# One common power for the three normalisations of an attention step on GpSimd

## What is computed

```python
def _layernorm(x, axis=-1, eps=1e-05):
    m = jnp.mean(x, axis=axis, keepdims=True)
    v = jnp.var(x, axis=axis, keepdims=True)
    return (x - m) / jnp.sqrt(v + eps)

x = x + _L0_attn_ref(_layernorm(x), ...)        # 16 heads of 8, queries = keys = values
x = x + _L0_xattn_ref(_layernorm(x), ctx, ctx)  # scores / sqrt(8), softmax over 64 keys
x = x + _L0_ffn_ref(_layernorm(x), ...)         # 7 experts, top 1, and a shared one
```

## Time and profile before

| | |
|---|---|
| median of three runs | 415.33 us (414.82 to 415.68) |
| span of the profiled execution | 427.0 us |
| PE busy | 404.4 us (95%) |
| DVE busy | 305.1 us (71%) |
| ACT busy | 298.5 us (70%) |
| POOL busy | 284.8 us (67%) |
| attention pipeline, full | about 40 to 222 us |
| drain of the attention, routing | about 222 to 270 us |
| experts | from 270 us on |

### The profile page before, as it was taken

The page is one execution under the profiler, slowest core; times in us unless marked ns, Lnnn a source line. Parts: engine busy times, 40 slices in busy tenths (PEclk is TensorE's granted clock), DMA queues, the critical chain, the costliest instruction groups (busy, mean ns, idle before and its releaser), DMA issues.

```text
span 427.0 us, 16199 instructions
## 1 busy us (share of the span) xinstructions
PE 404.4 (95%) x5545; PEld 312.9 (73%) x5546; DVE 305.1 (71%) x791; ACT 298.5 (70%) x684; POOL 284.8 (67%) x476
## 2 busy tenths in 40 slices
PE   7989999999998999999999898969999999999997
PEld 4646666666665666666665667959988999999996
DVE  7868999999998998999999787713333444444444
ACT  7659999999998999999998685302213466666651
POOL 8757788878887888888888423665664463444442
PEclk9999999999999999999999999996999999999999
DMA  6254566767676667765444300021113255430001
GB/s 104 43 85 64 87 103 108 109 110 121 120 124 117 114 123 126 143 101 84 60 63 43 35 2 2 27 81 58 69 69 90 67 133 139 131 104 27 27 32 52
DMA packets 176324, 35.22 MB, mean 82 GB/s; under 512 B 145587, under 2 KB 174646, under 8 KB 176256
## 3 DMA queue, kind: packets, MB, share of 16 engines
q1 hardware_dynamic: 71296, 21.43, 23.1%
q10 hardware_dynamic: 102144, 6.81, 15.2%
q0 software_dynamic: 2816, 6.10, 4.1%
HBM read 20.86 MB, written 15.67 MB: 86 GB/s over the span
## 4 chain that ended last, share of the span: by engine, by line
PE 68%; DMA 10%; issue 6%; DVE 6%; ACT 3%; SPq 2%; POOL 2%; another core or an unknown queue 2%; DVEq 0%; ACTq 0%; POOLq 0%
PE psum L867 15%; PE psum L659 12%; PE psum L668 12%; PE psum L973 8%; PE psum L680 7%; DMA orow<-attention_out 3%; DMA attention_out<-on_s 3%; PE psum L690 3%; SPq L198 2%; DMA ring<-sorted_rows 2%; PE psum L763 2%; PE psum L802 2%; PE psum L758 1%; PE psum L809 1%
## 5 line engine op out<-in xcount | busy, mean ns | idle before, releaser
L1583 DVE TENSOR_TENSOR gT<-gT,psum 128x384 f32<-128x384 f32 x66 | 36.5, 553 | 77.5 <-PE psum L867 34.4
L1263 ACT ACTIVATE gT<-psum 128x384 f32<-128x384 f32 x70 | 33.6, 488 | 58.4 <-PE psum L867 36.9
L620 POOL DMA_INDIRECT out<-yrow,token x38 | 37.1, 975 | 41.2 <-DVE yrow L1718 22.0
L973 PE MATMUL psum<-wdn_sb,gT 128*128 (+1 forms) x420 | 60.2, 280 | 4.0 <-DVE rows_all L1597 2.2
L479 POOL TENSOR_TENSOR k_s<-pT,hmask_sb 128x1024 f32<-128x1024 f32 x32 | 61.0, 1906 | 0.9 <-ACT pT L1137 0.8
L973 PEld LDWEIGHTS psum<-wdn_sb,gT 128*128 128x128 f32 x420 | 53.3, 195 | 5.7 <-issue 2.7
L867 PE MATMUL psum<-fhT,wtile 128*128 128x128 f32 x456 | 57.2, 275 | 0.3 <-ACT wtile L1292 0.3
L867 PE MATMUL psum<-hT_all,wup_sb 128*128 128x128 f32 x384 | 50.9, 283 | 5.0 <-issue 3.8
L867 PEld LDWEIGHTS psum<-fhT,wtile 128*128 128x128 f32 x456 | 53.9, 192 | 0.5 <-ACT wtile L1292 0.5
L867 PEld LDWEIGHTS psum<-hT_all,wup_sb 128*128 128x128 f32 x384 | 47.7, 198 | 6.0 <-issue 4.8
L1065 ACT ACTIVATE pr_x<-pr_x,rs 128x512 f32<-128x512 f32 x60 | 43.0, 722 | 8.2 <-DVE pr_x L1368 7.0
(11 more groups left out here) (193 smaller groups left out, 872.0 us busy)
## 6 DMA issues: line engine op xcount, KB each, us to landing
sorted_rows<-nowhere_row SPq DMA_DIRECT2D x38, 130.0 KB, 3.6
ring<-sorted_rows SPq DMA_DIRECT2D x30, 130.0 KB
wup_sb<-in_wup SPq DMA_DIRECT2D x14, 176.0 KB, 3.0
orow<-attention_out SPq DMA_DIRECT2D x31, 64.0 KB
ring<-in_ctxv ACTq DMA_DIRECT2D x60, 32.0 KB, 3.7
cross_keys<-in_ctxk ACTq DMA_DIRECT2D x14, 128.0 KB, 3.7
ring<-cross_keys SPq DMA_DIRECT2D x112, 16.0 KB
rows_all<-in_x ACTq DMA_DIRECT2D x10, 128.0 KB, 3.9
```

The lines of the kernel that those rows point to most:

```text
L620: pool.indirect_dma_start(out=out, out_offset=bass.IndirectOffsetOnAxis(ap=token[p][:, 0:1], axis=0), in_=yrow[p][:, :], in_offset=None, b ...
L973: last = nc.tensor.matmul(ps_y[p], gT[place_of(n) if isinstance(n, int) and n < FIRST else p][:, c, :], wdn_sb[:, expert, c, :], start=(c ...
```

## The change

The three norms share one addition of epsilon and one power on POOL, both over three columns. The s column has its place in the common one in the step in which DVE makes its variance ("pv_x" of POOL's step), which is later in POOL's order than the separate pair stood by one common block. The separate ve and power of s (L503, L508) leave the step, and with them the factor 8 in the variance: xn_s is multiplied by 8 ** -0.5 instead, in the same instruction. nmean leaves too: L450 becomes (row - mean) * rs, reading the mean in `mv`. ACT's cross exponential waits for the common power. DVE's variances wait for the uses of the same pair two units before, since the mean is now read to the end. In the drain one of the hand-written powers takes s along (unit 28), the last three units keep powers of their own, and the buffer numbers follow.

```diff
-        mhalf = sb("mhalf", [P, 2])
+        mhalf = sb("mhalf", [P, 3])
-        nmean = [sb(f"nmean{i}", [P, 3]) for i in range(2)]
@@ normed
-                nc.gpsimd.tensor_scalar(dst, x_all[:, u, :], nmean[i][:, NORM[k]:NORM[k] + 1], rs[i][:, NORM[k]:NORM[k] + 1],
-                                        ALU.add, ALU.mult).then_inc(sem(f"{k}_xn"), 1)
+                nc.gpsimd.tensor_scalar(dst, x_all[:, u, :], mv[i][:, NORM[k], 0:1], rs[i][:, NORM[k]:NORM[k] + 1],
+                                        ALU.subtract, ALU.mult).then_inc(sem(f"{k}_xn"), 1)
@@ POOL body
+                if live("norm"):
+                    pool.wait_ge(sem("p_mv"), at(u["norm"]))
+                if live("st_x"):
+                    pool.wait_ge(sem("x_mv"), at(u["st_x"]))
+                if live("pv_x"):
+                    pool.wait_ge(sem("s_mv"), at(u["pv_x"]))
+                nc.gpsimd.tensor_scalar(ve[:], mv[i][:, :, 1], EPS, None, ALU.add).then_inc(sem("px_ve"), 1)
...
-                    nc.gpsimd.tensor_scalar(nmean[i][:, 1:3], mv[i][:, 1:3, 0], -1.0, None, ALU.mult).then_inc(sem("px_mean"), 1)
...
+                if u["pv_x"] >= 2:
+                    pool.wait_ge(sem("x_exp"), G * (u["pv_x"] - 1))
+                pool.wait_ge(sem("px_ve"), px_turn(t))
+                nc.gpsimd.tensor_tensor(rs[i][:], ve[:], mhalf[:], ALU.pow).then_inc(sem("px_rs"), 1)
...
-                    nc.gpsimd.tensor_scalar(xn["s"][:], x_all[:, u["q"], :], mv[i][:, 0, 0:1], None,
-                                            ALU.subtract).then_inc(sem("s_xn"), 1)
+                    nc.gpsimd.tensor_scalar(xn["s"][:], x_all[:, u["q"], :], mv[1 - i][:, 0, 0:1], float(DK) ** -0.5,
+                                            ALU.subtract, ALU.mult).then_inc(sem("s_xn"), 1)
...
-                    nc.gpsimd.tensor_scalar(ve[:, 0:1], mv[i][:, 0, 1:2], EPS, float(DK), ALU.add, ALU.mult).then_inc(sem("s_ve"), 1)
...
-                    nc.gpsimd.tensor_tensor(rs[i][:, 0:1], ve[:, 0:1], mhalf[:, 0:1], ALU.pow).then_inc(sem("s_rs"), 1)
@@ POOL drain, roots_x
+                nc.gpsimd.tensor_scalar(ve[:, columns], mv[i][:, columns, 1], EPS, None, ALU.add).then_inc(sem("px_ve"), 1)
...
-            roots_x(33, U - 6)
+            roots_x(33, U - 6, U - 4)
             finish_x(33, U - 6)
-            centred(U + 1, U - 3)
-            root_s(33, U - 3)
+            centred(34, U - 3)
+            root_s(34, U - 3)
@@ ACT exp
-                if k == "x":
-                    act.wait_ge(sem("s_rs"), at(u))
+                if k == "x" and u < U - 3:
+                    act.wait_ge(sem("px_rs"), px_turn(u + LAG["pv_x"]))
+                elif k == "x":
+                    act.wait_ge(sem("s_rs"), u - (U - 3) + 1)
@@ DVE mean_variance
-                if k == "s" and u >= 2:
-                    dve.wait_ge(sem("s_ve"), u - 1)
-                    dve.wait_ge(sem("s_xn"), u - 1)
-                if k != "s" and t >= 2:
-                    dve.wait_ge(sem("px_ve"), px_turn(t - 2))
-                    dve.wait_ge(sem("px_mean"), px_turn(t - 2))
+                if u >= 2:
+                    dve.wait_ge(sem(f"{k}_xn"), u - 1)
+                if k == "s" and u == U - 1:
+                    dve.wait_ge(sem("s_ve"), 1)
+                elif 2 <= t < 39:
+                    dve.wait_ge(sem("px_ve"), min(px_turn(t - 2), px_turn(36)))
```

More of the change, by code:

```diff
@@ L455, in body @@
                 pool.wait_ge(sem("mv_set"), 2)
[L456 to L465, removed]
-                    nc.gpsimd.tensor_scalar(nmean[i][:, 1:3], mv[i][:, 1:3, 0], -1.0, None, ALU.mult).then_inc(sem("px_mean"), 1)
[L467 to L472, removed]
+                if live("norm"):
[5 more added lines that the diff above has]
+                nc.gpsimd.tensor_scalar(ve[:], mv[i][:, :, 1], EPS, None, ALU.add).then_inc(sem("px_ve"), 1)
+                if u["norm"] >= 2:
+                    pool.wait_ge(sem("p_xn"), min(u["norm"] - 1, U))
+                if u["st_x"] >= 2:
+                    pool.wait_ge(sem("x_xn"), u["st_x"] - 1)
+                if u["pv_x"] >= 2:
+                    pool.wait_ge(sem("x_exp"), G * (u["pv_x"] - 1))
+                pool.wait_ge(sem("px_ve"), px_turn(t))
+                nc.gpsimd.tensor_tensor(rs[i][:], ve[:], mhalf[:], ALU.pow).then_inc(sem("px_rs"), 1)
+                pool.wait_ge(sem("px_rs"), px_turn(t))
                 if live("norm"):
@@ L529, in add_x, with roots_x @@
                                         on["x"][:].rearrange("p a c d -> p (a c d)"), ALU.add).then_inc(sem("x_x"), 1)
-            def roots_x(t, u):
-                i = t % 2
+            def roots_x(t, u, crossed=None):
+                i, columns = t % 2, slice(1 if crossed is None else 0, 3)
                 pool.wait_ge(sem("x_mv"), at(u))
-                nc.gpsimd.tensor_scalar(ve[:, 1:3], mv[i][:, 1:3, 1], EPS, None, ALU.add).then_inc(sem("px_ve"), 1)
+                if crossed is not None:
+                    pool.wait_ge(sem("s_mv"), at(crossed))
+                nc.gpsimd.tensor_scalar(ve[:, columns], mv[i][:, columns, 1], EPS, None, ALU.add).then_inc(sem("px_ve"), 1)
                 pool.wait_ge(sem("p_xn"), U)
                 pool.wait_ge(sem("x_xn"), u - 1)
-                nc.gpsimd.tensor_scalar(nmean[i][:, 1:3], mv[i][:, 1:3, 0], -1.0, None, ALU.mult).then_inc(sem("px_mean"), 1)
+                if crossed is not None:
+                    pool.wait_ge(sem("x_exp"), G * (crossed - 1))
                 pool.wait_ge(sem("px_ve"), px_turn(t))
-                nc.gpsimd.tensor_tensor(rs[i][:, 1:3], ve[:, 1:3], mhalf[:], ALU.pow).then_inc(sem("px_rs"), 1)
+                nc.gpsimd.tensor_tensor(rs[i][:, columns], ve[:, columns], mhalf[:, columns], ALU.pow).then_inc(sem("px_rs"), 1)
             def finish_x(t, u):
                 pool.wait_ge(sem("px_rs"), px_turn(t))
-                pool.wait_ge(sem("px_mean"), px_turn(t))
                 normed("x", t, u, h_all[:, u, :], None)
@@ L1549, in _ @@
             moments_s(U - 1)
[L1550 to L1551 removed]
+            mean_variance("s", 36, U - 1)
+            centred(36, U - 1)
             soften_both("s", U)
```

43 lines of the change are left out of this document (18 added, 25 removed).

## The result

The kernel after the change takes 419.56 us (median of 4 runs, 418.70 to 420.02), the kernel before takes 415.50 us beside it (414.82 to 415.93). The ratio is 1.0101, with an interval of 1.0082 to 1.0119: slower by 4.1 us. My forecast was no change, at 415.6 us, and 419.56 lies outside the range of 414.4 to 417.9. What happened is the slower rival, to which I had given a chance of 0.22: the loop through k_s has become the bound.

The account below looks back on a forecast made before the run. PE, busy without a gap, bounds the attention steps; the k_s loop grows 0.22 to 7.00 us, under 7.05, so steps add nothing. The start adds 0.3: 415.33 + 0.3 = 415.6 us, range 414.4 to 417.9.

Parts of the forecast that it names:

- the slower rival: Attention steps: the new form is too long and k_s bounds; mostly 416.5 to 418.5 us, up to 421.6; chance 0.22.
- the loop through k_s: PE's scores through DVE's x variance and POOL's k_s back to PE: 6.78 of 7.05 us, growing 0.22 to 7.00.
- the three meetings: Points in each step where POOL's results are wanted: k_s (cover 0.27 us), query xn_s (0.56), ACT's x exponential (2.7 early).
- The exponential meeting: ACT's x exponential: its scale, made with the common power, ends near 111.1, still 2.7 us early, costing nothing.
- Removing the separate ve and power: POOL between xn_s and the next common ve: 0.76 us goes into waiting for mv; ve starts no earlier, counted 0.
- The hand-over from ve to the power: POOL between ve and k_s: with nmean gone, ve to power takes about 0.40 us instead of 0.50, change -0.10.
- The three-column power: POOL's power between ve and k_s: 0.89 us on three columns against 0.730 on two, change +0.16.
- The price of xn_p: POOL's subtract-and-multiply before k_s: 0.610 us against 0.452, change +0.16, ends +0 and +0.42.
- The new wait: POOL's common ve also waits for the s variance, which DVE issues ahead of the x variance: counted at 0.
- the far end: Upper end of the slower rival: each of about 25 steps grows 0.21 us, 5.3 in all, plus 1.0 at start: 421.6.
- The residual sum almost without idle time: POOL before xn_s: the residual sum comes 0.38 us later, using up most of its 0.46 us of idle time.
- The query edge: PE's load of xn_s: cover 0.56 us, of which 0.18 is left; holds at the middle values, breaks at the upper end.

Follow-up runs that it names:

- The idle additions: Kernel before with small 128x1 additions on POOL between the power and xn_p in steps 6 to 31: four took 434.66 us, two 428.66, against 428.40.
- the form alone: Kernel before with (row - mean) * rs in both normalisations and nmean removed, powers still apart: 414.69 us, ratio 1.0004.
- the probe: Kernel before with 28 extra GpSimd tensor_scalar instructions (14 forms, each twice) ahead of its first step: span 433.6 us.
- the factor 1.0: Kernel before with xn_s as (row - mean) * 1.0 instead of row - mean: 426.93 us, ratio 1.0007.
- p in the add form: Changed kernel with nmean back and (row + nmean) * rs for p alone, x keeping subtract: 429.52 us, ratio 1.0054.
- its two halves: Kernel before with only the subtract form and no nmean, 414.69 us; changed kernel with nmean and add form back for p and x, 415.04 us.

## Why the prediction was wrong, step by step

**What bounds the kernel, and the three meetings: right.** The loop over k_s with a cover of 0.27 us was the place. The idle additions put the cover at 0.29. The exponential meeting cost nothing, as said.

**Removing the separate ve and power starts nothing earlier: right.** They became POOL's idle time before ve, 0.86 us against a forecast of about 0.9.

**The hand-over from ve to the power: right.** 106.87 - 106.45 = 0.42 (0.40 in the kernel with the form alone), predicted 0.40.

**The three-column power: right.** 0.880 us, predicted 0.89; with its hand-over xn_p starts 0.98 us after the power, before 0.84.

**The price of xn_p: this step failed.** I took 0.61 (+0.16) because that row shared the operation and the operand with the new form; it took 0.806 (+0.36 by the distance to k_s, 108.62 - 107.85 = 0.77 against 111.53 - 111.12 = 0.41). The value lay within my bounds (up to 0.87), and I had written where it would decide: at 0.66 us. The mistake was to take the length of a lone subtract for that of a pair with a subtract. The probe shows that the 0.61 comes from there being one operation (an add alone takes as long) and that the pair is 0.20 us longer still; the row could not price the new form either way, and I took a second operation behind a subtract as free. The size of this one term turns the forecast over. With 0.36 in its place the sum is -0.10 + 0.16 + 0.36 = +0.42, beyond the cover: a step of about 7.20.

**The new wait, counted at 0: wrong by 0.08.** DVE does make the s variance long before, but the wait for it stands last in POOL's queue. That is the rest: +0.08 - 0.08 + 0.14 + 0.36 = +0.50, and the step is 7.27.

**From steps to the total.** Over the 26 steps from the sixth scores to the last, 0.21 x 26 = 5.5 us of growth is to be expected. The sums of these steps are 186.58 and 188.22 us in the two profiles of the kernel before and 190.48 after, +2.3 to +3.9. The kernel before pays 3 to 4.7 us for late transfers above 26 x 7.06 = 183.6, the changed one 1.5 above 26 x 7.27 = 189.0: it looks as if a longer step lets part of the transfers arrive in time. The other profiles point the same way, without proving it: the probe, the factor 1.0 and the two idle additions, all with steps of 7.06 to 7.08, have 1.8 to 2.5 us above 26 x 7.06, and the three other kernels with steps of 7.26 to 7.38 have 0.9 us or less above 26 of theirs. PE's first scores are 0.53 us later (10.05 against 9.52), where I had +0.44 at that place and +0.3 in the sum. Together this is 2.8 to 4.4 us, and the timed runs say 4.1. The rival's own scale (5.3 us for the far end) left this relief out.

**The residual sum almost without idle time: right,** it has none left. The query edge is closed too, and with xn_s itself 0.10 us longer. By itself it would set the step to about 7.14 (p in the add form), so it is second to k_s.

**Open.** In the kernels with the common power and a constant in xn_s, xn_s starts 0.10 us behind the end of the residual sum (112.06, 112.16); in the kernel before, in the one with the factor 1.0 there, and in those where the factor sits in ACT's copy, it follows at once. Neither the second operation nor the other buffer of the mean does it alone. I did not isolate it, nor what the constant's value has to do with it.

## What to carry to other kernels

Before taking an instruction out of an engine, measure the loop that its result closes, not the engine's load: here POOL lost three instructions a step and the kernel lost 4 us, since the price went into the only stretch with 0.29 us to spare, and neither half of the change was visible alone. When a new form of instruction lies on such a stretch and no row has that form, the nearest row is no price for it: here the middle value and the far bound fell on two sides of the cover, so the form should be timed by itself before the change is judged. On GpSimd a mean negated once and then added (0.45 us) was cheaper than a mean subtracted ahead of a multiplication (0.81). Put waits that have long been fulfilled ahead of the one that ends last.

## What the runs showed of the hardware

- GpSimd's tensor_scalar on 128x128 fp32: add with multiply 0.45 us (0.37 with a constant as the second operand), one operation alone 0.60 (0.53 by a constant), subtract in a pair 0.80 (0.72 with a constant, 0.65 with two). A second operation can make it shorter: add alone took 0.61, add with multiply 0.45.
- Its power on 128 rows took 0.57, 0.73 and 0.88 us for one, two and three columns: one power for three norms is cheaper than two by 0.42 us, but all of it lies where the first result is wanted.
- A semaphore wait that is fulfilled already costs 0.07 to 0.08 us behind the wait that ends last, and nothing to be seen ahead of it.
- PE's weight load starts 0.05 us after the end of the POOL result that it waits for.
- The same kernel took 414.8 us on one chip and 426 to 428 on others. All eight profiles of the slower ones, and the recorded one of the kernel before, have a gap at the beginning of the experts: in 270 to 300 us PE was busy for 24.4 to 26.6 us at a mean granted clock of 0.89 to 0.94, against 29.2 to 30.0 at 1.00 in the profiles of the changed kernel, of its two halves and of the kernel before, taken again, on faster ones. In the recorded profile PE first stood idle at full clock (1.48 us busy from 282 to 286 us), and only then did the granted clock fall (0.75 from 286 to 290). So the clock is not the beginning of that gap; what is remains open. The attention steps were alike on all.
